# ScalarE's order in a windowed-attention pipeline: Gelu in the second slot of a step, and the attention copy between the copies of turned queries and keys

## The reference, cut to what matters

```python
for i in range(DEPTH):                                   # 6
    x = attn_layer(shift_tokens(x), Wqkv[i], q_scale[i], k_scale[i], Wo[i]) + x
    x = ffn_layer(shift_tokens(x), ln_g[i], ln_b[i], W1[i], b1[i], W2[i], b2[i]) + x

def attn_layer(x, Wqkv, qs, ksc, Wo):
    q, k, v = jnp.split(x @ Wqkv, 3, -1)                 # 16 heads of 64
    q = l2norm(q) * qs ;  k = l2norm(k) * ksc            # then the rotary turn of both
    out = local_attention(q, k, v)                       # window 32, looks one window back, softmax
    return out @ Wo

def ffn_layer(x, g, bln, W1, b1, W2, b2):
    hg = layernorm(x) * g + bln @ W1 + b1
    a, gate = jnp.split(hg, 2, -1)                       # 341 wide each
    return a * gelu(gate) @ W2 + b2
```

## Time and profile before

| what | value |
|---|---|
| median of 3 runs | 1858.72 us (1857.57 to 1862.71) |
| the profiled execution's own time | 1855.56 us |
| its span | 1853.8 us, 68588 instructions |
| PE busy | 1663.1 us (90%) |
| DVE busy | 1430.3 us (77%) |
| ACT busy | 1344.7 us (73%) |
| POOL busy | 1293.3 us (70%) |
| chain that ended last, by engine | PE 68%, ACT 11%, issue 10%, DVE 9%, POOL 1% |
| granted TensorE clock, mean | 0.978 |

### The profile page before, as it was taken

One profiled execution on the slowest core, in us unless ns is written; L12 is line 12 of the kernel. 1 busy time (PEld: TensorE's weight loads), 2 busy tenths in 40 slices (PEclk: granted clock), 3 DMA queues, 4 the chain that ended last, 5 costly groups with the idle time before them and its releaser, 6 DMA issues.

```text
span 1853.8 us, 68588 instructions
## 1 busy us (share of the span) xinstructions
PE 1663.1 (90%) x25968; PEld 1291.5 (70%) x26160; DVE 1430.3 (77%) x3041; ACT 1344.7 (73%) x2656; POOL 1293.3 (70%) x1283
## 2 busy tenths in 40 slices
PE   7889999999999999999999999999999999999973
PEld 5667777777777777677777777767777776777751
DVE  4588878878778787887778778788777777778755
ACT  4267777777777777777777777777777777777753
POOL 5287777777777777777777777777777777677720
PEclk9799999999999999999999999999999999999995
DMA  5011111111101011110111101111110111101000
GB/s 164 11 38 34 32 33 32 30 40 48 32 28 34 28 41 46 33 30 28 34 45 41 34 28 30 31 47 37 33 34 29 33 37 32 30 24 30 25 14 20
DMA packets 41406, 66.13 MB, mean 36 GB/s; under 512 B 7072, under 2 KB 16032, under 8 KB 41376
## 3 DMA queue, kind: packets, MB, share of 16 engines
q1 hardware_dynamic: 40224, 65.38, 11.7%
q10 hardware_dynamic: 1152, 0.34, 0.1%
HBM read 20.61 MB, written 1.05 MB: 12 GB/s over the span
## 4 chain that ended last, share of the span: by engine, by line
PE 68%; ACT 11%; issue 10%; DVE 9%; POOL 1%; ACTq 1%; DMA 0%; DVEq 0%
PE ps_a L490 11%; PE ps_f L490 11%; PE ps_qs L490 9%; PE ps_po L490 8%; PE ps_q L490 7%; PE ps_k L490 5%; PE ps_v L490 5%; PE ps_po L604 4%; PE ps_qs L596 3%; PE ps_tk L596 3%; ACT L906 2%; DVE ssq L1084 2%; DVE prob L1121 2%; ACT p_bd L838 2%; ACT squares L844 2%
## 5 line engine op out<-in xcount | busy, mean ns | idle before, releaser
L426 POOL TENSOR_TENSOR qk<-qk,rnorm 128x512 f32<-128x512 f32 x384 | 393.1, 1045 | 298.2 <-DVE rnorm L1111 298.2
L418 POOL TENSOR_TENSOR qk<-qk,qk_rot 128x512 f32<-128x512 f32 x384 | 483.7, 1276 | 111.1 <-DVE qk_rot L1078 110.8
L1084 DVE TENSOR_REDUCE ssq<-squares 128x8 f32<-128x512 f32 x384 | 257.6, 680 | 71.1 <-ACT squares L844 58.2
L490 PE MATMUL ps_qs<-k_t,q_t 64*32 64x64 f32 x12288 | 210.7, 218 | 67.6 <-ACT k_t L838 46.5
L838 ACT COPY p_bd<-ps_po 64x512 f32<-64x512 f32 x384 | 221.3, 576 | 34.7 <-PE ps_po L604 32.4
L433 POOL TENSOR_TENSOR prob<-prob,row_inv 128x512 f32<-128x512 f32 x192 | 200.3, 1043 | 51.5 <-DVE row_inv L1130 51.5
L1127 DVE TENSOR_REDUCE row_sum<-prob 128x8 f32<-128x512 f32 x192 | 131.7, 686 | 120.6 <-ACT prob L944 120.6
L490 PEld LDWEIGHTS ps_qs<-k_t,q_t 64*32 64x32 f32 x12288 | 179.7, 107 | 57.2 <-issue 57.2
L944 ACT ACTIVATE prob<-prob 128x512 f32<-128x512 f32 x192 | 121.2, 631 | 110.9 <-DVE prob L1121 107.6
L490 PEld LDWEIGHTS ps_po<-p_bd,v_back 128*64 128x64 f32 x3072 | 162.9, 137 | 49.5 <-issue 31.8
L490 PE MATMUL ps_po<-p_bd,v_back 128*64 128x64 f32 x3072 | 193.9, 225 | 1.6 <-ACT p_bd L838 1.5
(11 more groups left out here) (161 smaller groups left out, 4002.6 us busy)
## 6 DMA issues: line engine op xcount, KB each, us to landing
v_back<-v_own SPq DMA_DIRECT2D x192, 192.0 KB, 2.4
w_raw<-in_wqkv SPq DMA_DIRECT2D x48, 192.0 KB, 2.4
v_back<-v_own SPq DMA_DIRECT2D x96, 64.0 KB, 2.1
wo_sb<-in_wo SPq DMA_DIRECT2D x12, 256.0 KB, 3.0
w_sb<-in_w SPq DMA_DIRECT2D x6, 341.0 KB, 3.4
w_sb<-in_w SPq DMA_DIRECT2D x6, 192.0 KB, 2.7
x_in<-in_x SPq DMA_DIRECT2D x4, 256.0 KB, 5.0
out<-s_out SPq DMA_DIRECT2D x8, 128.0 KB, 1.9
```

Of the source, the lines that this page charges most:

```text
L418: nc.gpsimd.tensor_tensor(qk[:, s, i, :], qk[:, s, i, :], qk_rot[:, s, i, :], ALU.add).then_inc(added, 1)
L426: nc.gpsimd.tensor_tensor(heads(qk[:, s, i, :]), heads(qk[:, s, i, :]), rnorm[:, s, 8 * i:8 * i + 8].unsqueeze(2).to_broadcast([P, 8, HEAD ...
L490: return nc.tensor.matmul(o, lhs, rhs, start=start, stop=stop, **kw)
L1084: V.tensor_reduce(ssq[:, s, 8 * i:8 * i + 8], heads(squares[:, s, OCTET * i:OCTET * i + OCTET]), AX, ALU.add).then_inc(ssq_done, 1)
```

## The change

It touches ScalarE's program alone. `keep_turned` is split in two, `keep_attention` moves from the end of a slot to between them in the next slot, Gelu (with its table load) moves from the end of slot 0 to slot 1 behind the copy of the turned keys, with `keep_p` right behind it, and in the other slots `keep_p` stands behind both squares (in slot 0 it stood between them).

```diff
-            def keep_turned(u, j, s):
-
-                octet, tile = j // 2, j % 2
+            def keep_queries(u, s):
+
                 wait(act, s_done, u - 1)
                 act.wait_ge(tq_done, u + 1)
                 copy(q_t[:, s, :], ps_qs[:]).then_inc(q_turned, 1)
+
+            def keep_keys(u, j):
+
+                octet, tile = j // 2, j % 2
                 act.wait_ge(tk_done, u + 1)
                 copy(k_t[:, octet, :, WINDOW + P * tile:WINDOW + P * tile + P],
                      ps_tk[:].rearrange("p (c t) -> p c t", t=P)).then_inc(k_turned, 1)
...
                     if live(u - 2):
-                        keep_turned(u - 2, (j - 2) % UNITS, j % 2)
+                        keep_queries(u - 2, j % 2)
+                    if live(u - 4):
+                        keep_attention(u - 4, n - 1, j)
+                    if live(u - 2):
+                        keep_keys(u - 2, (j - 2) % UNITS)
+                    if j == 1 and live_batch(n - 3):
+                        gelu(n - 3)
+                        if live(u - 3):
+                            keep_p(u - 3, (j - 3) % 2)
                     if live(u):
                         squares_of(u, 0, j % 2)
-                    if j == 0 and live(u - 3):
-                        keep_p(u - 3, (j - 3) % 2)
-                    if live(u):
                         squares_of(u, 1, j % 2)
-                    if j > 0 and live(u - 3):
+                    if live(u - 3) and not (j == 1 and live_batch(n - 3)):
                         keep_p(u - 3, (j - 3) % 2)
...
                     if live(u):
                         keep_v(u, n, j)
-                    if live(u - 3):
-                        keep_attention(u - 3, n if j >= 3 else n - 1, (j - 3) % UNITS)
-                    if j == 0 and live_batch(n - 3):
-                        gelu(n - 3)
```

## The result

The changed kernel takes 1884.22 us, median of 4 runs (1881.38 to 1887.16), beside 1859.95 for the kernel before on the same chip (4 runs, 1857.57 to 1862.71). The ratio is 1.013, 95% interval 1.0107 to 1.0153: slower by 1.3%. The forecast was 1884.0, slower with 0.80. The profiled execution took 1887.16 us; its span is 1885.4, against 1853.8 before.

What follows compares the result with a forecast made beforehand. Bound: TensorE to slot 0's `less_max`, then ScalarE's gapless run, slot 1's `less_max`, `xn`, `ff_down`. 45 passes x 0.57 = 26 us, against the median of 1858.72, gave 1884 us; range 1864 to 1896.

Steps and rivals of the forecast that it cites:

- The bound: Loop closed by TensorE to slot 0's `less_max`, ScalarE's gapless run, slot 1's `less_max`, `xn`, `ff_down`; scores' 1.00 us wait beside it.
- The gain of 0.86: Slot 1: scores follow the turned probabilities at once, near 929.15 instead of 930.01, putting TensorE 0.86 us ahead.
- Slot 1, Gelu ahead of `p_bd` and the squares: ScalarE's second table load starts 0.57 us late, delaying `less_max`, `xn` and `ff_down`; the pass is 0.57 us longer.
- the estimate by that page: Adding the Trainium skill's drain to the second table load: 1.82 us a pass, 82 us in all; given no chance.
- Slot 0, the late `p_bd`: `p_bd` behind both squares makes `values` 0.58 us late, mostly absorbed before the turn; keys turned about 0.06 us later.
- The rival with the late `p_bd`: Slot 0's delay is not absorbed: keys up to 0.24 us later, 0.75 us or more a pass, 1893 us; chance 0.08.
- The sum: 45 passes x 0.57 = 26 us, the last steps adding nothing: 1884 us against the median.
- The three last steps: After the loop, one table load of 1.28 us goes where ScalarE waits for others anyway: worth nothing.
- What would show it: Signs expected in the changed profile's waits on TensorE, ScalarE and VectorE, and a pass of 36.3 us.
- Only the turn binds: `xn` has slack, so only 0.16 to 0.25 us at slot 2's turn counts: 1866 to 1870 us; chance 0.12.
- Faster: Early scores let slot 1's `less_max` end before TensorE is ready: pass 0.86 us shorter, 1820 us; chance 0.11.

Runs made afterwards that it cites:

- e1: Kernel before, with Gelu moved behind slot 1's copies of queries and keys, its table load staying at the end of slot 0: 1857.15 us.
- e7: Kernel before, with values' copy of slot 0 early and Gelu behind slot 1's copies of queries and keys, its load ahead: 1837.39 us.
- e2: Kernel before, with the copy of the projected values in slot 0 moved ahead of Ln and the small Exp: 1834.73 us.
- e3: Kernel before, with `xn` made ahead of the first rotation of slot 2 on VectorE: 1871.76 us.
- e6: Changed kernel, with only `p_bd` of slot 0 put back between the two squares: 1876.15 us.
- e4: Kernel before, with only the attention copy moved between the next slot's copies of turned queries and keys: 1859.52 us.
- e5: Changed kernel, with Gelu and its load back at the end of slot 0 and `p_bd` behind both squares in every slot: 1850.0 us.
- e12: Kernel before, with values' copy of slot 0 early and, in slot 2, `xn` and `x_run` first; Gelu and its load unmoved: 1825.24 us.
- e10: Changed kernel, with `xn` ahead of slot 2's first rotation and `x_run` ahead of its sums of squares: 1853.26 us.
- e9: Kernel before, with `xn` ahead of slot 2's first rotation and `x_run` ahead of its sums of squares: 1850.77 us.
- e8: Kernel before, with values' copy early, Gelu behind slot 1's copies with its load ahead, and `xn` and `x_run` first in slot 2: 1805.57 us.

## Why the prediction was right, point by point

**The bound.** Right that the wait before the scores was worth nothing (e1, e7), though it was read as 1.00 us where 0.69 of it was idle time: "1.85 us, which is the 10.23 less 8.38" holds because both sides lack the same record. The gain of 0.86 was taken by starts and came out as 0.85. Right that ScalarE's run to `less_max` was (e2: 0.47 us for a copy of 0.47). The last link was named wrongly. The path runs "without slack through Exp, sums and first rotation to `xn`", I wrote, and everything that follows is TensorE's own stream; the runs showed it goes on through the second rotation, the squares of the keys on ScalarE and their sums to `x_run` and `ff_up`. This cost no size, since the stretch is equally long in both kernels: from `less_max` to `x_run` is 6.99 us in both (940.49 - 933.50, and 960.98 and 953.98 give 7.00), so `ff_up` moved by what `less_max` moved by. It would have cost one had I been asked for e3, and there it did.

**Slot 1, Gelu ahead of `p_bd` and the squares.** From the end of the keys' turn to `less_max` the prediction has 934.07 - 927.18 = 6.89 us; measured 953.98 - 947.12 = 6.86, where before it was 6.38. The second switch of tables took 1.28 us for the load, and 0.61 from the squares' start to the load (0.62 said). By the Trainium skill (ScalarE: Activation LUTs, What ACT_TABLE_LOAD costs) some 1380 ns of drain should come on top of the load; the load agrees with the trace, the drain does not show in it, and the loss was 24 us and not the 82 of the estimate by that page.

**Slot 0, the late `p_bd`.** The term was mis-sized. I said 0.06 us a pass, with 0.24 kept for the range. Measured, from the large Exp of slot 3 to the turned keys is 10.67 us (936.45 to 947.12) against 10.48 (916.64 to 927.12): 0.19, and e6 gives 0.19 back. `p_bd` started 5.32 us behind that Exp, not 5.25 (941.77 - 936.45; 921.89 - 916.64), since the squares ahead of it were released 0.10 and not 0.03 behind the rotation; and `values` starts 0.14 behind the end of `p_bd` (941.77 + 1.16 to 943.07), where I took 0.07. So two distances from a release to the next start were taken 0.07 us too short each. These 0.14 went through to the turn whole, because its slack, 0.45 us by starts (924.88 - 923.63 less 0.80), was used up by the 0.58 already in the sum. The rival with the late `p_bd` (up to 0.24) was thus in good part true.

**The sum.** A pass longer by 0.69, not 0.57: 0.12 too little, or 5 us in 45 passes. The three last steps I had put at nothing. The last loop pass begins, by its first projection, here; first before, then after:

```profile
1737.37 0.50 PE L490 MATMUL ps_q<-w_hi,xs_hi 128*128 x1
```

```profile
1772.93 0.49 PE L490 MATMUL ps_q<-w_hi,xs_hi 128*128 x1
```

From there to the end of the span, less one pass, is 80.7 us before (1853.8 - 1737.37 - 35.70) and 76.1 after (1885.4 - 1772.93 - 36.39): 4.6 us the other way. The attention copy brings 1.8 of it (78.9 in e4 and in e5), and the other 2.8 came with Gelu's place; whether they are the table load that is no longer issued was not tested. The granted clock of that last stretch does not explain it: at 0.69 it is 80.2 us in e12, 78.9 in e4 and e5 and 76.7 in e10. The first loop pass begins at 172.35 in the profiled execution after and at 166.84 before, but VectorE's two moves put that point 5.6 us later in e9 (172.47) and 4.6 earlier in e10 (167.72), so I do not count it to the change; the granted clock up to it is 0.89 after and 0.92 before. 45 passes of 0.69 less 4.6 are 26 us; the medians are 24 apart, and runs of one kernel differ by 5. That 1884.0 meets 1884.2 so closely is therefore luck: two errors of 5 us that cancel. The sign and the mechanism were foreseen, and the size to within these errors.

**What would show it.** No wait for `k_t`, a hole of 0.4 on ScalarE, the load 5.0 behind the keys' copy, 1 us at the turn, a plain wait for `xn`, `values` behind `p_bd`, 36.3 us a pass: all there, with 0.0, 0.45, 4.93, 1.01, 0.45, 0.62 and 36.4. One was wrong, and of the wrong sign: VectorE's idle time before `rn_a` was to grow, and shrank from 0.84 to 0.18 us. The prediction's own numbers said so: the maximum done near 933.8, `rn_a` at 933.97. The squares come so late that VectorE stands before the sums instead, 2.82 us where it was 1.03: the two waits together are longer (3.00 for 1.87), but most of it lies earlier.

**Against the rivals.** "Only the turn binds" is excluded by e10 (1853 and not 1884). "Faster" needed `less_max` of slot 1 done before TensorE was ready for the turn; it ends at 954.67 (953.98 + 0.69), and the turn starts at 954.73 after 1.01 us of idle time.

## What to carry to other kernels

When a wait of the bounding engine looks like a prize, follow the loop round once from the wait behind it: here the wait before the scores was worth 0 alone (e1), 0 beside one other repair (e7), and 20 us once `xn` and `x_run` came early too (e8 against e12). Count the records first: a wait can hold an instruction that the trace lacks. Look for every pair in which one engine starts a fixed small distance behind another's end, and not only for the first; here the last one closed the loop (`x_run`, not `xn`). In a gapless run, first take out what can stand in an idle place earlier on the same engine (e2), before its order is changed.

## What was not expected of the hardware

A matmul group can wait for another engine while the view marks no wait. The projection matmuls have rows of 0.39 or 0.40 us and follow each other after 0.23, so a start that is up to 0.17 late leaves no gap in the view. In the kernel before, `ff_down` starts 0.47 behind the last of them and e3 shows that 0.32 is enough: 0.15 us a pass. `ff_up` starts 1.21 behind the scores, where 1.03 is enough: 0.18, of which 0.11 lies between the rows (940.98 to 941.09) and is not marked either. Together they hid 0.33 us a pass, of which e9 brought 0.22 back.

A table load costs its 1.28 us and the wait for the end of the instruction ahead of it. Behind a copy or squares that wait is some 0.13 us (0.61 from start to start, for 0.47 to 0.49 otherwise); behind `p_bd` it is nothing, since the load follows its start by 1.19 (930.41 to 931.60) and so do the squares (920.70 to 921.89).
